# Second FFN of a four-block layer on one core: two chunks issued ahead of the second row's turn, and the eight banks dealt out anew

## The reference, cut to what matters

```python
x = x + mixer(layernorm(x))       # recurrence and gated MLP
x = x + ffn(layernorm(x))         # first FFN    (f = 0)
x = x + attention(layernorm(x))   # 16 heads over 1024 tokens
x = x + ffn(layernorm(x))         # second FFN   (f = 1): where the change is

def ffn(h):                                     # h: 2 rows x 1024 tokens x 128
    logits = h @ gate_w.T + gate_b              # 8 experts
    scores = softmax(logits); top_v, top_i = top_k(scores, 2)
    out = 0
    for e in range(8):
        gate = (top_i == e).sum(-1) * top_v.sum(-1)
        inter = h @ wi.T + bi + (h @ lora_A[e].T) @ lora_B[e].T     # 512 wide
        out += gate[..., None] * (relu(inter) @ wo.T + bo)
    return out
```

## Time and profile before

| | us |
|---|---|
| median of 3 runs | 663.77 (663.32 to 664.48) |
| the profiled execution's own time | 665.23 |
| its span, first to last instruction | 663.4 |
| PE busy in it | 607.7 (92%) |
| DVE busy in it | 520.3 (78%) |
| ACT busy in it | 378.1 (57%) |
| mean granted TensorE clock, share of full | 0.98 |

### The profile page before, as it was taken

One profiled execution on the slowest core, in us unless ns is written; L12 is line 12 of the kernel. 1 busy time (PEld: TensorE's weight loads), 2 busy tenths in 40 slices (PEclk: granted clock), 3 DMA queues, 4 the chain that ended last, 5 costly groups with the idle time before them and its releaser, 6 DMA issues.

```text
span 663.4 us, 9240 instructions
## 1 busy us (share of the span) xinstructions
PE 607.7 (92%) x3304; PEld 243.5 (37%) x3304; DVE 520.3 (78%) x939; ACT 378.1 (57%) x696; POOL 110.5 (17%) x140
## 2 busy tenths in 40 slices
PE   7978899999989799899999998999999988998997
PEld 5454445544466362122222122222222212335443
DVE  5676867854768988997997989999999996339634
ACT  3945123332501206786887777888888889962331
POOL 5940120100104552013012000000100011011000
PEclk9999999999989799999999999999999999997999
DMA  7100000000221211201101010010010000000001
GB/s 230 57 1 0 1 0 1 0 1 0 97 73 39 95 66 39 83 2 57 63 17 41 3 31 27 2 49 8 24 35 3 1 2 0 1 1 0 14 19 32
DMA packets 18989, 20.22 MB, mean 30 GB/s; under 512 B 3968, under 2 KB 12672, under 8 KB 18944
## 3 DMA queue, kind: packets, MB, share of 16 engines
q1 hardware_dynamic: 16900, 18.55, 8.9%
q10 hardware_dynamic: 1388, 0.50, 0.3%
q0 software_dynamic: 656, 0.59, 0.3%
HBM read 15.23 MB, written 4.19 MB: 29 GB/s over the span
## 4 chain that ended last, share of the span: by engine, by line
PE 65%; DVE 20%; ACT 6%; DMA 3%; issue 2%; DVEq 2%; ACTq 1%; POOL 0%; POOLq 0%; SPq 0%
PE banks L1600 17%; PE banks L1586 13%; DVE negmax L1167 9%; PE banks L1513 7%; PE banks L1303 6%; PE banks L1385 5%; PE banks L1376 3%; ACT arena L859 3%; PE banks L1428 3%; PE banks L1316 2%; PE banks L1646 2%; PE banks L1528 1%; DVE arena L1074 1%; DVE arena L1019 1%; ACT arena L849 1%
## 5 line engine op out<-in xcount | busy, mean ns | idle before, releaser
L1167 DVE TENSOR_REDUCE negmax<-banks 128x2 f32<-128x1024 f32 x256 | 301.4, 1220 | 25.0 <-PE banks L1513 21.5
L859 ACT ACTIVATE arena<-banks 128x512 f32<-128x512 f32 x512 | 268.0, 606 | 84.0 <-PE banks L1586 83.0
L1586 PE MATMUL banks<-arena 59*128 59x512 bf16 x512 | 148.5, 382 | 7.3 <-ACT arena L859 5.8
L1513 PE MATMUL banks<-arena 56*128 56x512 bf16 x512 | 121.3, 390 | 19.7 <-DVE negmax L1167 17.6
L1600 PE MATMUL banks<-arena 128*32 128x512 f32 x1024 | 136.4, 605 | 0.6 <-ACT arena L859 0.6
L1586 PEld LDWEIGHTS banks<-arena 59*128 59x128 bf16 x512 | 37.8, 94 | 151.3 <-ACT arena L859 135.7
L1385 PE MATMUL banks<-arena,bT 128*128 128x512 f32 x128 | 60.1, 593 | 1.5 <-ACT arena L697 1.5
L575 POOL TENSOR_TENSOR rstd<-veps,neghalf 128x4 f32<-128x4 f32 (+1 forms) x24 | 27.1, 1129 | 199.8 <-DVE veps L933 154.6
L697 ACT ACTIVATE arena<-banks 128x512 f32<-128x512 f32 (+1 forms) x56 | 32.2, 597 | 47.3 <-PE banks L1316 19.3
L1513 PEld LDWEIGHTS banks<-arena 56*128 56x128 bf16 x512 | 26.0, 93 | 68.2 <-DVE negmax L1167 60.8
L1019 DVE TENSOR_SCALAR arena<-banks,bi 128x512 f32<-128x512 f32 x32 | 23.9, 746 | 33.0 <-PE banks L1385 33.0
(11 more groups left out here) (148 smaller groups left out, 652.2 us busy)
## 6 DMA issues: line engine op xcount, KB each, us to landing
arena<-qk_scratch SPq DMA_DIRECT2D x124, 48.0 KB
arena<-in_tab SPq DMA_DIRECT2D x4, 1024.0 KB, 6.9
qk_scratch<-arena SPq DMA_DIRECT2D x8, 384.0 KB, 2.6
out<-x SPq DMA_DIRECT2D x4, 256.0 KB, 2.3
arena<-qk_scratch SPq DMA_DIRECT2D x62, 16.0 KB
x<-in_x POOLq DMA_DIRECT2D x1, 512.0 KB, 8.4
arena<-nm_part SPq DMA_DIRECT2D x32, 4.0 KB, 1.8
x<-in_x SPq DMA_DIRECT2D x1, 256.0 KB, 3.4
```

Source lines behind the costliest of these rows:

```text
L859: act.activation(probs[s % 2][:, h, :], score_bank(g, n), ACT.Exp, scale=SCALE).then_inc(exp_done, 1)
L1167: return dve.tensor_reduce(negmax[:, buf, keys, :, at_tile], slot, axis=AXX, op=ALU.max, negate=True)
L1513: last = pe.matmul(slot[:, side, :], qs[rows, buf, pair, t * P:(t + 1) * P], ks[rows, buf, pair, keys * HALF:(keys + 1) * HALF], start=Tru ...
L1586: pe.matmul(score_bank(g, n), ks[rows, g % BUFS, pair, t * P:(t + 1) * P], qs[rows, g % BUFS, pair, q * HALF:(q + 1) * HALF], start=True, ...
```

## The change

The banks of the second FFN are dealt out anew, two `base` calls are issued ahead of the turn of row 1, that row's logits come in three jobs (3, 3 and 2 tiles) where there were four of two, and dummy matmuls stand ahead of both T1.1 jobs.

```diff
-BUSY = {N_REC: (14, 3), N_MLP: (7, 10)}
+BUSY = {N_REC: (14, 3), N_MLP: (7, 10), N_FFN1: (11, 2)}
 def token_tiles(f, b):
-    return [(0, 1, 2), (3, 4, 5), (6, 7)] if (f, b) == (1, 0) else [(t, t + 1) for t in range(0, NT, 2)]
+    return [(0, 1, 2), (3, 4, 5), (6, 7)] if f == 1 else [(t, t + 1) for t in range(0, NT, 2)]
 IN_LAST_GROUP = {...
-                 "X1.0.1.0": 6, "X1.0.1.1": 7, "T1.1.0": 2, "T1.1.1": 3, "U1.1.0": 6, "U1.1.1": 7, "U1.1.2": 2, "U1.1.3": 3}
+                 "X1.0.1.0": 6, "X1.0.1.1": 7, "T1.1.0": 6, "T1.1.1": 7, "U1.1.0": 0, "U1.1.1": 1, "U1.1.2": 4, "O1.0.0": 5, "R1.0.0": 5,
+                 **{f"{x}1.0.1.{c}": c + 2 if c < 2 else c + 4 for x in ("HA", "HB") for c in range(FC)}}
             def flip_norm(n, b, prefix):
                 for h in range(2):
-                    if (n, b) in ((N_REC, 0), (N_MLP, 0)):
+                    if (n, b) in ((N_REC, 0), (N_MLP, 0), (N_FFN1, 1)):
                         keep_busy(f"{prefix}.{b}.{h}", BUSY[n][h])
                         if (f, q) == (1, 1):
                             pe.wait_ge(ring_emptied, ring_at(GROUPS - 1, len(RING_LAST)))
+                            base(f, q, 0)
+                            base(f, q, 1)
                             flip_norm(N_FFN1, 1, f"T{f}")
                             logits(f, 1)
-                        base(f, q, 0)
-                        base(f, q, 1)
+                        else:
+                            base(f, q, 0)
+                            base(f, q, 1)
```

## The result

The changed kernel takes 666.04 us (median of 20 runs, 663.24 to 668.13), the kernel before 663.39 (20 runs, 662.33 to 665.62). The ratio is 1.0037, 95% interval 1.0026 to 1.0048: slower by 2.65 us at the medians, beyond the 0.2% that this kernel's measurement can tell. Forecast were 665.8 and +2.0, range 663.6 to 667.8. In us the interval of the difference is 1.7 to 3.2.

A forecast was written before the change was run, and what follows sets the result against it. PE was taken to bound the kernel, its arrival at O1.0.1 deciding the end. A lead of 2.5 lost whole to the wait, +0.4 beyond it and +1.5 for the clock gave +1.9 on 663.77, said as 665.8; range 663.6 to 667.8.

The forecast's parts named there:

- Two bases ahead: Ahead of row 1's turn: two bases run 600.78 to 602.50 in PE's idle time, taking 1.72 from behind the logits.
- Dummies: Ahead of T1.1.0: eleven dummy matmuls end at 604.92, 1.0 later than the norm's first half allows; overshoot costs 0.2.
- Logits: Row 1's logits: full clock, but banks shared with the sums; they end at 609.06, 0.6 earlier than 609.67.
- Lead at O1.0.0: Start of O1.0.0 after block 1's chunks: 614.2 against 616.69, so PE leads by 2.5.
- The wait: Second base of block 2 waits for bank 5 until add_ffn of block 0 ends, 623.25 to 626.1: 2.85.
- The sum at full clock: At O1.0.1: 632.1 against 631.74, the lead of 2.5 lost whole and 0.4 with it.
- The clock in the gap: Behind the block 2 wait: the clock falls to half, costing 1.5 for the shorter low stretch, 3.1 for the longer.
- the shorter stretch: Low-clock stretch of at least 3.30 behind the block 2 gap: costs 1.5; the forecast case, chance 0.40.
- Transposes at full clock: At row 1's turn: four transposes take 0.44, following the trace; by the skill they would stay near 0.9.
- The median: Whole kernel: 663.77 + 1.9 = 665.7, given as 665.8, the median taken 1.46 below the profiled time.
- the case without a fall: Rival: the block 2 wait comes but the clock stays up; 664.2, no measurable difference, chance 0.29.
- the longer stretch: Rival: half clock behind the block 2 gap for at least 6.70, costing 3.1; 667.3, chance 0.20.

The follow-up runs named there:

- Experiment 6: Changed kernel with bank turns reordered so no block 2 job waits for R1.0.0, and without the 13 dummies ahead of T1.1; 661.40 us, ratio 0.9970.
- Experiment 1: Changed kernel with only the bank turns behind R1.0.0 reordered, so no block 2 job waits for R1.0.0; 662.06 us, ratio 0.9982.
- experiment 2: Kernel before with banks 1 and 7 swapped behind R1.0.0, adding only the late wait of HA1.1.0.1; 668.10 us, ratio 1.0065.
- experiment 3: Changed kernel with 12 dummy matmuls issued in the block 2 gap, the wait kept; 664.29 us, ratio 1.0024.
- Experiment 4: Kernel before with only dummies added, 14 ahead of T1.1.0 and 2 ahead of T1.1.1; 663.06 us, ratio 0.9999.
- experiments 4 and 5: The latter: kernel before with 16 dummies, three logits banks, an own bank for O1.0.0 and R1.0.0, new turns, no base ahead; 661.82 us, ratio 0.9978.
- experiment 8: Changed kernel with banks dealt to avoid the late wait and logits sharing with sums, without the 13 dummies; 659.66 us, ratio 0.9944.

## Why the prediction was right, and where its sizes were off

The direction, the place and the mechanism hold, step by step. One step, the fall of the clock, held as a chance and not as something that the rows could tell.

- *Two bases ahead*: 600.74 to 602.46, forecast 600.78 to 602.50. Right.
- *Dummies*: T1.1.0 at 604.91, forecast 604.92. Experiment 6 confirms that the overshoot is worth nothing here.
- *Logits*: end forecast 609.06, measured 609.17, the last job behind bank 4's sum as said.
- *Lead at O1.0.0*: forecast 2.5, measured 2.33.
- *The wait*: 2.85 forecast, 2.69 idle (2.85 from the end of the step ahead, 623.35, to 626.20). Experiment 1 takes the loss away by removing this wait alone, experiment 2 brings it into the kernel before by adding it alone.
- *The sum at full clock*: forecast +0.4, measured +0.6 in experiment 3. The logits' 0.1 and the first base behind the wait (0.96 to the next row and not 0.86) make up most of the 0.2.
- *The clock in the gap*: forecast to fall, for the shorter stretch, at 1.5. It fell in both profiled executions of the changed kernel, for the shorter stretch, at 1.7. In the one of experiment 2 it did not, so the chance that I kept for it was due. It also did not fall "right behind" the gap: the first base ran at 1.00. The forecast weighed a fall behind 2.99 and 1.96 against none behind 2.09, each read from one execution. The last two readings were luck: behind the same idle times of 1.96 and 2.09, in code that no kernel here changes, other executions went the other way (see the last section).
- *Transposes at full clock*: four took 0.44 start to start at 604.91. The Trainium skill (TensorE: Matmul & The Clock Gate, Part 4: PE-mode transpose) has them stay out of the full clock. The trace after differs from it as the one before did.
- *The median*: 666.04 against 665.8, the difference 2.65 against 2.0. Part of the close hit is luck: the kernel before came out at 663.39 in 20 runs, 0.38 below the 663.77 of the first three that the sum started from.

One sentence was wrong: that the kernel before loses up to 2.1 less where the clock stays up at the turn. Experiment 4 gives 0.5, because O1.0.0 would then have waited for DVE's picking. I looked only for the banks that were waited for in the trace, not for those that would be with PE 2 us ahead. The forecast was spared by it, as the term only made me lean high. The same oversight hid what the split into three jobs and the bank of its own were worth: 1.6 of stretch between experiments 4 and 5.

Two sums were off a little. The chances for slower and same add up to 0.60 and 0.33, not 0.61 and 0.32. And the range does not follow from its own bounds: -0.4 lies 0.8 below the case without a fall, not 0.6, and 667.8 lies 0.5 above the longer stretch without a reason given. Neither matters for 666.04.

## What to carry to other kernels

When work is pulled forward on one engine, list for every later bank its last reader and when that reader can be done. There are two kinds. A reader that hangs on the pulled work itself comes forward with it, so its wait is as long with the lead as without: 2.69 idle in the changed kernel and in experiment 2. A reader that hangs on something else stays where it is and eats the lead: in experiment 4 DVE's picking ended 16.1 into the stretch as before, and of a lead of 2.1 it left 0.6 at O1.0.0 (16.14 against 16.78).

In a round of banks the job that is emptied last should be followed last. The Trainium skill (PSUM — Partial Sum Buffer, Summary: rules for kernel authors) says to evacuate promptly. The trace agrees, with 2.69 idle for one bank that was emptied late. This case adds that the order of reuse counts too: another order of the same eight banks took 4.6 us off the stretch.

A gap on TensorE is to be priced twice, once for its length and once for the matmuls behind it. Here the wait alone cost 3.0 (experiment 2), of which the lead left 0.6, and the half clock behind it 1.7 where it came.

## What was unexpected of the hardware

- The same idle time does not give the same clock. Two gaps of the MLP lie in code that none of these kernels changes. Behind the one of 1.95 to 1.96 the clock was at 0.50 in 5 of the 12 profiled executions (before among them). Behind the one of 2.09 to 2.10 it was at 0.50 in 10 of 12, and the trace of before is one of the two where it stayed at 1.00. In the changed kernel's trace the second gap reads:

```profile
60.25 2.61 PE L1304 MATMUL banks<-arena,w_outT 128*128 128x512 f32 x3 [2.09 <-DVE arena L1099]
```

```profile
60.60:63.40 2.80, 2.80 (x4) 1.01 (x3) 2.58 (x5) 0.73 (x2) 0.00 (x0) 0.50 0.00 0
```

- The same holds at the places changed here. Behind 2.69 the clock stayed at 1.00 in experiment 2, and in both profiles of the changed kernel it fell, about 1 us after work had begun again. With 1.21 or 1.22 and 0.59 idle and eight transposes between and behind them it fell in experiment 8 and stayed up in experiment 6. One trace can't say which it will be.
- The part of the program that no kernel here touches ended at 595.8 to 600.2 in different executions. Differences of 2 us in a single time say nothing here; those within the stretch repeated to 0.1 (65.8 and 65.8, 60.4 and 60.3).
